# One timetable over all 32 images in place of a loop over iterations, with an order of its own for each engine

## The reference: two metaformer layers on 32 images

```python
# layer 0
x = x + conv0(ln_c(x))          # conv0: 1x1 expand 96->576, bn, silu; 3x3 depthwise, bn, silu;
                                # gate from the pooled means (two small products, sigmoid);
                                # 1x1 project 576->96, bn; plus conv0's own input
t = tokens(x); t = t + ffn(ln_t(t), W1, b1, W2, b2)      # 96 -> 384 -> 96, values rounded to
                                                         # fp8 e5m2 before, fp16 after each product
# layer 1
x = x + conv1(ln_c(x))          # 1x1, group norm over the whole image, gelu; four axially shifted
                                # copies, each 1x1 and gelu, summed; group norm; 1x1
t = tokens(x); t = t + ffn(ln_t(t), W1, b1, W2, b2)
```

## Time and profile before

| | us |
|---|---|
| median of 3 runs | 8133.32 |
| the runs | 8124.04 to 8137.58 |
| the profiled execution | 8123.94 |
| its span, first to last instruction | 8122.1 |

### The profile page before, as it was taken

One profiled execution on the slowest core, in us unless ns is written; L12 is line 12 of the kernel. 1 busy time (PEld: TensorE's weight loads), 2 busy tenths in 40 slices (PEclk: granted clock), 3 DMA queues, 4 the chain that ended last, 5 costly groups with the idle time before them and its releaser, 6 DMA issues.

```text
span 8122.1 us, 110800 instructions
## 1 busy us (share of the span) xinstructions
PE 6148.7 (76%) x40192; PEld 2370.1 (29%) x40192; DVE 5512.9 (68%) x9325; ACT 4740.2 (58%) x7907; POOL 568.9 (7%) x366
## 2 busy tenths in 40 slices
PE   2777778778778778778778777777787787787775
PEld 1223223333223333223233233332233332232221
DVE  5666777666776666776667776667766667766664
ACT  1455665655656556656556656556565566565555
POOL 0000000000000000000000000000000000000000
PEclk8888888888889888888888898888898888898887
DMA  1222322323322323322223223223223233232222
GB/s 40 51 70 65 82 72 60 76 62 73 82 64 64 77 63 76 81 54 72 71 67 80 74 60 75 64 70 84 68 60 77 62 75 81 54 72 72 64 65 61
DMA packets 395480, 556.40 MB, mean 69 GB/s; under 512 B 71491, under 2 KB 391428, under 8 KB 391772
## 3 DMA queue, kind: packets, MB, share of 16 engines
q1 hardware_dynamic: 394940, 549.32, 27.8%
HBM read 233.66 MB, written 78.68 MB: 38 GB/s over the span
## 4 chain that ended last, share of the span: by engine, by line
PE 41%; DVE 29%; ACT 11%; DMA 9%; issue 7%; SPq 3%; POOL 0%; DVEq 0%; ACTq 0%; POOLq 0%
DVE conv L828 14%; PE bank L552 9%; PE bank L526 5%; PE bank L567 5%; PE b_banks L632 4%; PE bank L505 4%; DMA r_b<-rstd_row_c 4%; PE bank L554 3%; PE b_banks L651 2%; DMA r_b<-rstd_row_b 2%; ACT L779 2%; PE bank L642 2%; PE b_banks L587 2%; DMA r_a<-rstd_row_a 2%; DVE hidden L880 1%
## 5 line engine op out<-in xcount | busy, mean ns | idle before, releaser
L828 DVE SCALAR_TENSOR_TENSOR conv<-mid,w_dw,conv 128x1568 f32<-128x1568 f32 x1536 | 2830.6, 1843 | 14.1
L505 PE MATMUL bank<-xc_a,w_exp 128*128 128x392 f32 x1536 | 827.1, 638 | 463.3 <-DVE xc_a L811 423.4
L967 POOL TENSOR_TENSOR x<-x,xc_a 96x392 f32<-96x392 f32 x256 | 551.3, 2153 | 7042.4 <-DVE xc_a L811 7042.4
L587 PE MATMUL b_banks<-xn,w_q 128*128 128x392 fp8e5 x1536 | 390.1, 368 | 714.1 <-DVE xn L872 672.5
L632 PE MATMUL b_banks<-shifted,w_combo 128*32 128x392 f32 x6144 | 748.3, 540 | 31.8 <-DMA shifted<-g 31.0
L552 PE MATMUL bank<-conv,w_proj_gated 128*96 128x392 f32 x2048 | 760.2, 516 | 0.0
L744 ACT ACTIVATE hidden<-b_banks 128x1176 f16<-128x1176 f32 x512 | 589.9, 1152 | 208.8 <-PE b_banks L587 207.3
L851 DVE SCALAR_TENSOR_TENSOR x<-bank,bn_bias,r_a 96x392 f32<-96x392 f32 x256 | 159.2, 622 | 812.0 <-PE bank L554 812.0
L567 PE MATMUL bank<-x,centering 128*96 128x392 f32 x1536 | 653.4, 517 | 61.7 <-ACT sq_b L663 43.3
L751 ACT ACTIVATE hidden<-hidden 128x1176 fp8e5<-128x1176 f16 x512 | 608.1, 1188 | 33.7 <-DVE hidden L880 30.9
L662 ACT ACTIVATE g<-bank 96x392 f32<-96x392 f32 x512 | 252.5, 493 | 589.2 <-PE bank L567 320.9
(11 more groups left out here) (158 smaller groups left out, 8718.6 us busy)
## 6 DMA issues: line engine op xcount, KB each, us to landing
phases_on<-phases SPq DMA_DIRECT2D x768, 101.5 KB, 2.2
shifted<-g SPq DMA_DIRECT2D x512, 149.6 KB, 2.8
r_b<-rstd_row_b SPq DMA_DIRECT2D x512, 147.0 KB, 2.9
shifted<-g SPq DMA_DIRECT2D x256, 199.5 KB, 2.9
x<-in_x SPq DMA_DIRECT2D x32, 1176.0 KB, 7.8
r_a<-rstd_row_a SPq DMA_DIRECT2D x256, 147.0 KB, 3.4
x_plus_norm<-x SPq DMA_DIRECT2D x256, 147.0 KB, 2.1
r_a<-x_plus_norm SPq DMA_DIRECT2D x256, 147.0 KB, 2.2
```

What stands on the lines that cost most here:

```text
L505: mm(ring[bank][:, 0:TW], WEXP[:, 128 * k:128 * k + 128], xc_tile(t, 128), start=True, stop=True)\
L587: last = mm(PB[:, c, 0:TW], W1Q[:, f, 128 * c:128 * c + 128], XN8[t % 2][:, :], start=True, stop=True)
L828: v.scalar_tensor_tensor(out=acc, in0=src, scalar=WDW[:, k, j:j + 1], in1=acc, op0=ALU.mult, op1=ALU.add).then_inc(sem["convolved"], 1)
L967: g.tensor_tensor(tile(XA, t), tile(XA, t), xc_tile(t), ALU.add).then_inc(sem["xplus_a"], 1)
```

## The change

The iteration is given up. `timetable` gives each engine a list of its own, over all 32 images: step `s` of image m stands at PERIOD * m + time, where the time is a number in `TIMES` for that engine, step and tile. So the order of two steps may differ from engine to engine, and the steps of one image reach into a neighbour's without a boundary. The numbers set the order alone; nothing waits for a time. `with_banks` no longer takes banks in turn: a ring step gets the bank whose reader stands earliest in the readers' lists. Beyond that, `expand` and `texp` wait on `normed_a` for their tile in all cases, and `x1` of the last image waits for the stores of the image whose buffer it fills. No instruction's shape is changed, and the compute instructions of an image are the same in number but for table loads.

```diff
-    dw10=(1.3, 16.3), dw11=(14.6, 30.6), dw20=(31, 46), dw21=(46, 62), dw00=(66, 81.9), dw01=(91.1, 97.8),
-def schedule(do_a, do_b, do_e, do_next):
...
-    return [step for _, step in sorted(plan, key=lambda p: p[0])]
+PERIOD = 10000
+TIMES = {
...
+    "DVE": {
+        "rstd_a": (6141,), "norm_a": (6569, 6723, 6864, 7166, 7202, 7462, 7998, 8010),
...
-def with_ring(steps, last):
-
-    last = {bank: (s, back + 1) for bank, (s, back) in last.items()}
-    out = []
-    bank = 0
-    for s in steps:
-        if s[0] in USES_RING:
-            bank = (bank + 1) % RING
...
+def timetable():
+
+    plan = {engine: [] for engine in TIMES}
+    for engine, families in TIMES.items():
+        for family, times in families.items():
+            name, *index = family.split()
+            for t, time in enumerate(times):
+                step = (name, *map(int, index)) if name in WHOLE else (name, *map(int, index), t)
+                plan[engine] += [(PERIOD * m + time, m - lead_of(family), step) for m in range(NIMG)]
+        plan[engine].sort()
+    return plan
+
+
+def with_banks():
...
+    free = {bank: bank - PERIOD * NIMG for bank in range(RING)}
...
+        if step[0] in USES_RING:
+            bank = min(free, key=lambda b: free[b])
+            prev = last[bank]
+            last[bank] = (step, i)
+            reader = ("x1", step[1]) if step[0] == "proj" else step
+            bank_of[i, reader] = bank
+            free[bank] = read_at[i, reader]
...
             elif name == "expand":
                 k, t = arg
-                if k == 0:
-                    pe.wait_ge(sem["normed_a"], at(NT * n + t + 1))
-                wait_bank(pe, prev, i)
+                pe.wait_ge(sem["normed_a"], at(NT * (n if k < AHEAD else a) + t + 1))
+                wait_bank(pe, prev)
...
+                pe.wait_ge(sem["normed_a"], at(NT * a + (NT if h else NTH + 1)))
...
+                if not has_next:
+
+                    dve.wait_ge(stored[t], at(16 * (a - 1)))
```

More of the change, by code:

```diff
@@ L42 @@
 NQ = C // 32
-def spread(start, end, steps):
-    return [(start + (end - start) * (j + 0.5) / len(steps), s) for j, s in enumerate(steps)]
-def pipeline(start, end, *stages):
-    return [(start + (end - start) * t / (NT - 1) + lag, stage(t)) for t in range(NT) for lag, stage in stages]
-TIMES = dict(
-    dw10=(1.3, 16.3), dw11=(14.6, 30.6), dw20=(31, 46), dw21=(46, 62), dw00=(66, 81.9), dw01=(91.1, 97.8),
-    silu2=1.4, expand2=(2.8, 15.8), expand1=(67.2, 78.6), t0=(-5.1, 5, 10), t1=(13.6, 18, 24.6),
-    t2=(23, 28, 34), se=(69.6, 70.6, 71.6), proj=(74, 90), proj_lags=(1, 2, 5.6), rstd0=95.0,
-    ffn0=(18, 27.5), ffn0_lags=(0.4, 2, 4, 6, 8, 10), rstd1=41.3, conv1=(46, 55), conv1_lags=(0.8, 2.7),
-    gn0=58.3, gelu1=(57.3, 67.9), combos=(61.5, 76), combos_lags=(2, 4, 6), gn1=83, gn_weights=83.4,
-    conv3=(85.1, 90.7), conv3_lags=(1, 2, 4), rstd2=94.5, ffn1=(1.8, 12),
-    ffn1_lags=(1.0, 2.6, 4.6, 6.6, 7.6), load_x=20.1, center_a=(37.2, 44.3), center_a_lag=1.2, rstd_a=47.6,
-    norm_a=(51.0, 64), norm_a_lags=(0.5, 2), fetch=1.5)
@@ new lines @@
+LEAD = {
+    1: ("load_x", "center_a", "var_a", "rstd_a", "fetch_a", "norm_a", "save_s", "expand 0", "expand 1", "dw 0 0", "dw 0 1"),
+    0: ("expand 2", "dw 1 0", "dw 1 1", "dw 2 0", "dw 2 1", "silu2 0", "silu2 1", "silu2 2", "texp 0", "texp 1",
+        "texp 2", "tconv 0", "tconv 1", "tconv 2", "se1", "se2", "se3", "fetch_s", "proj", "x1", "center 0", "var 0",
+        "rstd 0"),
+    -2: ("fetch 2", "norm 2", "up 1", "quant 1", "down 1", "add 1", "store"),
+}
+WHOLE = ("load_x", "rstd_a", "rstd", "se1", "se2", "se3", "gn", "gn_weights")
@@ new lines, in with_banks @@
+def with_banks():
+    plan = timetable()
+    read_at = {(i, step): time for engine in ("DVE", "ACT") for time, i, step in plan[engine]
+               if engine == "ACT" or step[0] in ("x1", "se2")}
+    last = {bank: None for bank in range(RING)}
+    free = {bank: bank - PERIOD * NIMG for bank in range(RING)}
+    sums = {}
+    bank_of = {}
+    out = {"PE": []}
+    for _, i, step in plan["PE"]:
+        bank = prev = None
+        if step[0] in USES_RING:
[5 more added lines that the diff above has]
+            free[bank] = read_at[i, reader]
+        elif step[0] in ("var", "var_a") and step[-1] == 0:
+            which = "sums_a" if step[0] == "var_a" or step[1] == 0 else "sums_b"
+            prev = sums.get(which)
+            sums[which] = (step, i)
+        out["PE"].append((i, step, bank, prev))
+    for engine in ("SP", "ACT", "DVE", "POOL"):
+        out[engine] = [(i, step, bank_of.get((i, step)), None) for _, i, step in plan[engine]]
+    return out
@@ L663, in center_out @@
             f(sq, src, ACT.Square).then_inc(sem[s], 1)
-        for (name, *arg), bank, _ in steps:
+        for i, (name, *arg), bank, _ in plan["ACT"]:
+            a, b, e, n, parity = i, i - 1, i - 2, i + 1, i % 2
+            has_next = n < NIMG
             if name == "center_a":
```

194 lines of the change are left out of this document (65 added, 129 removed), and 53 rows, old and new, of the table TIMES.

## The result

| | before | changed |
|---|---|---|
| median, us | 8128.68 (4 runs, 8122.2 to 8137.58) | 7023.33 (4 runs, 7010.7 to 7025.62) |
| profiled span, us | 8122.1 | 7008.9 |

The ratio is 0.8636, with a 95% interval of 0.8621 to 0.8651. The forecast was 7450, its range 7080 to 7880.

What follows compares the result with a forecast made beforehand. No engine was full: a DVE-bound part, then an ACT and PE part where DVE mostly waits. Stages of 62 + 75 + 87 = 224 us a period against 246.2; 101.7 + 28 x 224 + 1076 = 7450 us, range 7080 to 7880.

Steps and rivals of the forecast that it cites:

- stage C: From the end of `dw 2 1` to the next `dw 0 1`, projections with second ffn: 26 + 53 + 8 = 87 us.
- PE's list: PE's work from the first projection to `var 0 7`: 46.6 us plus 6 us of waits, 53 us.
- the tail: After `var 0 7`: `rstd 0`, store and fetch, with only four short DVE steps beside them, 8 us.
- the rivals on the slow side: Gains given back where engines' orders cross, 7814 us, chance 0.22; PE at half clock beside conv1 and combos, 8813 us, 0.08.
- A: From `dw 0 1` to the end of `dw 1 0`, with the first ffn: 53.5 us of DVE work at 87%, 62 us.
- B: From `norm 1` to the end of `dw 2 1`: 61.7 us of DVE work, 71 at 87%, plus 4 wait, 75 us.
- the nine loads: ACT table loads between gelu and silu on the chain of waits, 4148 to 4183: worth 11 us a period at most.
- It is work of the kind of 4017 to 4137, so I take that stretch's 87%: DVE's busy share in the old dense stretch, depthwise convolution beside both ffns, applied to the first stage's 53.5 us: 62 us.
- the SP wait: `norm_a 0` waits for `rstd_a`'s store and fetch behind all eight shifts on SP: 4 us, bounds 0 and 21.
- The dense rival: Orders fit better, DVE at 95% in the first two stages: about 203 us a period, 6810 us (7024 at 210); chance 0.15.
- the rival of crossings: Engines with separate lists hold each other at steps reached later: 12 us a period back, 236, 7814 us; chance 0.22.
- The ramp and drain: The span outside setup and 28 equal periods gains half a steady period's share: 1126.8 to 1076 us.

Runs made afterwards that it cites:

- before_late_load: Kernel before with the image's load issued later (`load_x` 34.0 instead of 20.1), clear of the first ffn's fetches on SP: 8079.8 us, ratio 0.9928.
- the three runs: Kernel before, ACT's list alone moved by rule in the dense stretch: copies much later, phase copies slightly later, or `quant` earlier; 9712.8, 8705.3 and 8810.4 us.
- before_act_later: Kernel before, ACT alone taking `texp`, `tconv`, `down`, `center` and `expand` 0.8 to 1.2 time units later in the dense stretch: 9712.8 us, ratio 1.1955.
- after_rstd_early: Changed kernel with the store of `rstd_a` and its first two fetches moved ahead of shift 6 on SP: 7008.6 us, ratio 0.8613.

## Why the prediction was right, and where it failed

**The mechanisms of the moves were right.** Table loads: six an image. The x1 wait fell from 25.0 to 2.8 us. The new wait of `norm_a 0` behind the shifts stood where forecast; it was 7.4 us instead of 4. Combos came every (3178.73 - 3149.42) / 7 = 4.2 us, forecast 3.9:

```profile
3149.42 2.18 PE L663 MATMUL b_banks<-shifted,w_combo 128*32 128x392 f32 x24 [0.65 <-DMA shifted<-g]
...
3178.73 2.18 PE L663 MATMUL b_banks<-shifted,w_combo 128*32 128x392 f32 x24 [1.32 <-ACT gelus L810]
```

In stage C proj 0 started 25.4 us in (forecast 26), PE's list lasted from there to `rstd 0` at 3260.3, 50 us (53), and the tail 9.3 (8). In PE's list two errors nearly cancelled, which is luck: 46.6 us of work and 6 of waits were forecast, and there were 49.3 of busy PE and 0.9 of waits:

```profile
3210.10:3260.30 50.20, 49.27 (x259) 20.55 (x253) 34.04 (x67) 28.50 (x46) 0.00 (x0) 1.00 0.21 58
```

None of the rivals on the slow side came: PE's clock stayed at 1.00 in A and 0.93 in B. The 11 us that the forecast gave the nine loads at most is no term of its sum; without any loads but two the kernel before gained 2.7 a period.

**The step that failed** is "It is work of the kind of 4017 to 4137, so I take that stretch's 87%", for stages A and B. A's DVE work was summed to 53.5 us group by group, and the stage took 53.6. Part of that is a slip in the sum: neighbours of different groups overlap a little (a tap at 3269.59 lasts 1.03 us and the next instruction starts at 3270.53), so the stretch's busy time was 50.75, and the 87%, a share of busy time, was laid on a sum that counts the overlaps twice. At 87% A would have been 58.3; that leaves 4.7 us for the density itself. In B two errors met. Its other 65.0 us hold 60.5 of busy DVE, 93%, where 71 were taken, and the SP wait was 3.4 longer. In sum A is 8.4 below the forecast, B 2.6, C 2.1: 13.1 us a period, 28 x 13.1 = 367 us. The dense rival was the case that came, at the slow end of its 6810 to 7024, but that 7024 meets the measured 7023 is luck; its own sizes (56, 65, 80, which make 201 and not the 203 of the text) were too long for A and too short for B and C.

Why the density did not carry over has two parts. The first is read off the traces: an idle share belongs to the waits that stand in a stretch, not to the kind of work. Of DVE's 14.0 us of listed waits in the 120 before, these 10.3 were norms waiting for a fetched row:

```profile
DVE xn L872 <- DMA r_b<-rstd_row_c: 6.7, 3, 4.1
...
DVE xn L872 <- DMA r_b<-rstd_row_b: 2.0, 1, 2.0
DVE g L867 <- DMA r_b<-rstd_row_b: 1.6, 2, 1.4
```

A has none in the period shown. Over twelve images, from 2433.7 to 5386.6 before and from 2148.7 to 4673.4 in the changed kernel, DVE's waits for the rows of r_a and r_b were these before:

```profile
DVE xn L872 <- DMA r_b<-rstd_row_c: 87.5, 37, 5.4
DVE xc_a L811 <- DMA r_a<-rstd_row_a: 82.7, 37, 5.3
DVE xn L872 <- DMA r_b<-rstd_row_b: 26.2, 17, 3.0
DVE g L867 <- DMA r_b<-rstd_row_b: 23.1, 22, 1.9
```

and these in the changed kernel:

```profile
DVE xc_a L842 <- DMA r_a<-rstd_row_a: 95.9, 25, 8.8
DVE xn L906 <- DMA r_b<-rstd_row_b: 74.8, 25, 4.5
DVE xn L906 <- DMA r_b<-rstd_row_c: 26.8, 13, 2.9
DVE g L901 <- DMA r_b<-rstd_row_b: 24.5, 29, 2.0
```

They have not gone, 18.3 us a period before and 18.5 now, but they stand elsewhere. Those of `norm 0`, whose ffn is still A's, fell from 7.3 to 2.2 a period, and the one that is left stands ahead of the first tap, in C. Part of that is the place of the image's load, which no longer meets the row fetches of the first ffn (it is issued at 3084.90, the last of them at 3074.68): moving it alone in the kernel before took 3.4 (before_late_load). Those of `norm 2` grew from 2.2 to 6.2 and stand in C; in the period shown PE is busy throughout them.

The trace of before had a nearer stretch to read, too. It runs the same taps, `dw 0 1` and `dw 1 0`, with one ffn beside them, and there DVE was busy 92%:

```profile
3994.00:4049.50 55.50, 37.27 (x288) 14.33 (x287) 50.97 (x87) 37.26 (x59) 0.00 (x0) 0.85 0.20 52
```

At that share 50.75 us of busy DVE are 55 us, where 62 were forecast.

The second part is shown by experiment: that A is as dense as this hangs on ACT's order. With ACT in PE's order the stage takes 66 us, more than the 62 forecast. The forecast treated "each engine in its own order" as a way for steps to meet badly (the rival of crossings), and gave the order of ACT no price on either side.

PE's work in A was also mis-sized: 38 us "at full clock" were 46.9 of busy time at a clock of 1.00. A was closer to a PE bound than thought. That this is why 11.8 us of PE waiting for `quant` came through at once is argued, not shown.

**The ramp and drain** were to gain half of a steady period's share, 1126.8 to 1076. They took 7008.9 - 101.5 - 28 x 210.9 = 1002, 11% less against 14% of a period. From the last half chunk to the end it is 7008.9 - 6734.2 = 274.7 us, before 8122.1 - 7810.1 = 312.0. So 37 of the 125 us came from the drain, and the rest from the ramp, where the old iterations held back the few images there were by their boundaries. No experiment was made on that last cause; it is argued only. This is 74 us of the error, with the 367 together the 441 us by which the span lies below 7450.

**What the gain is made of.** 35.7 us a period. By the table above it is not in stage A: from `dw 0 1` to `dw 1 1` it took 55.2 us before and takes 55.6 now. It is in the three intervals of the moved work: 15.6 from `dw 0 0` to `dw 0 1`, though the second ffn has come into it, and 13.5 and 5.9 from `dw 1 1` to `dw 2 1`. Loads alone gave 2.7 in the old kernel, and putting twelve back cost 6.8 in the new. Taking the second ffn out of the projections costs 24.8, giving ACT PE's order 25.3. These prices don't add up to the gain; what the second one costs in A is no share of it, since the kernel before was as fast there with one order for all engines. A stretch is filled only if the work is there and its copies come in time.

PE's products are the same in number and shape, but were busy for less time. The page before:

```profile
PE 6148.7 (76%) x40192; PEld 2370.1 (29%) x40192; DVE 5512.9 (68%) x9325; ACT 4740.2 (58%) x7907; POOL 568.9 (7%) x366
```

Now it is 5784.1, 11.4 us less an image, at a mean granted clock of 0.943 against 0.865. No experiment tells this from the gain by the moves that keep PE busy.

**What stays open.** What it is in ACT's list that makes the phase copies and `quant` so sensitive in the kernel before: the three runs show the loss and the DVE and PE waits, but a longer wait for fetched rows (19.7 us in before_act_later) comes with them, and it was not told apart which of the two begins it. Open too is how near a common order made for the new places would come.

## What to carry to other kernels

Before you carry a stretch's busy share over to a new list, name the waits that make up its idle part and ask of each whether its step is still in the stretch: here 10.3 of 14.0 us belonged to norms waiting for a row, of which the new stage has none, and 87% became 95%. Look in the old trace for the stretch whose steps are nearest to the new one's: it stood at 92%. The order of an engine that is busy 60% of the time and that the main work waits on only now and then can cost as much as the placement of the main work brings: taking another engine's order for it cost 25 of 210 us here, and moving families a little by rule cost 7 to 20%. When several local repairs of visible waits each give nothing, as four did here, ask whether the next wait is as late as the one removed: in after_rstd_early it was.
